# A third decay buffer that lies in SBUF, and one butterfly stage of the weight transform made by Pool

## The reference

```python
# first block, per token t, channel d, state n
dA = exp(delta[t, d] * A[d, n])
h  = dA * h + (delta[t, d] * x[t, d]) * B[t, n]
y[t, d] = sum_n h[d, n] * C[t, n]
# second block
x = fwht(x * SU_ug) / 64
x_up   = x @ W_up.T   * (Wscale_ug[:2048] * 64)
x_gate = x @ W_gate.T * (Wscale_ug[2048:] * 64)
x = silu(x_gate) * x_up
x = fwht(x * SU_dp) / 64
x = x @ W_down.T * (Wscale_dp * 64)
```

## Time and profile before

| | us |
|---|---|
| median of 3 runs (2644.28 to 2645.57) | 2645.28 |
| the profiled execution | 2648.76 |
| its span, first instruction to last | 2647.0 |
| first scan starts, last scan starts | 70.7, 2466.7 |
| PE busy | 2574.1 (97%) |
| DVE busy | 2243.8 (85%) |
| POOL busy | 2046.4 (77%) |
| ACT busy | 1815.0 (69%) |

### The profile page before, as it was taken

How to read it: one execution, slowest core, us unless ns; L and a number is a source line. 1 busy time by engine, 2 the same in 40 slices (tenths; PEclk the granted TensorE clock), 3 DMA queues, 4 the chain that set the end, 5 groups by cost and what they waited for, 6 DMA issues and landing times.

```text
span 2647.0 us, 46296 instructions
## 1 busy us (share of the span) xinstructions
PE 2574.1 (97%) x16048; PEld 2187.0 (83%) x16048; DVE 2243.8 (85%) x2573; ACT 1815.0 (69%) x3935; POOL 2046.4 (77%) x1691
## 2 busy tenths in 40 slices
PE   7999989999999999999999999999999999989998
PEld 5566668989888888989888898989888898978888
DVE  6898998899898898899899889989889889889522
ACT  4776777677777777777777767777777777755322
POOL 6776879788787979888797979888797988877222
PEclk9999999999999999999999999999999999989999
DMA  5654256657666666666666665766666666646675
GB/s 181 214 204 167 100 166 219 224 196 241 210 236 215 216 221 209 238 204 232 220 224 221 215 225 199 240 212 227 225 216 221 207 221 214 224 176 230 239 288 190
DMA packets 165209, 564.41 MB, mean 213 GB/s; under 512 B 17264, under 2 KB 19696, under 8 KB 132976
## 3 DMA queue, kind: packets, MB, share of 16 engines
q1 hardware_dynamic: 164976, 561.44, 61.5%
HBM read 527.30 MB, written 34.08 MB: 212 GB/s over the span
## 4 chain that ended last, share of the span: by engine, by line
PE 78%; DVE 10%; ACT 7%; issue 3%; DMA 1%; POOL 0%; SPq 0%; DVEq 0%; ACTq 0%; POOLq 0%
PE pF L726 21%; PE hT L633 14%; PE pM L651 13%; PE pD L742 10%; PE pM L703 8%; DVE h L1180 5%; DVE acc L1193 3%; PE pM L673 3%; PE pD L766 3%; ACT decay L986 2%; PE decay L726 2%; PE hT L625 1%; PE pF L766 1%; ACT delta L963 1%; ACT delta L958 1%
## 5 line engine op out<-in xcount | busy, mean ns | idle before, releaser
L1180 DVE TENSOR_TENSOR_SCAN h<-decay,dbx 128x512 f32<-128x512 f32 x1024 | 1200.1, 1206 | 73.7 <-ACT decay L986 41.5
L1362 POOL TENSOR_TENSOR dbx<-u,bb 128x2048 f32<-128x2048 f32 (+1 forms) x272 | 1179.6, 4338 | 37.5 <-DVE h L1180 35.5
L986 ACT ACTIVATE decay<-delta,a_neg 128x255 f32<-128x255 f32 x2048 | 874.0, 468 | 301.8 <-DVE h L1180 295.0
L1193 DVE SCALAR_TENSOR_TENSOR acc<-hT,bcT,acc 128x1024 f32<-128x1024 f32 x480 | 610.3, 1271 | 141.1 <-PE hT L633 137.5
L726 PE MATMUL pF<-fxT_hi,wug 128*128 128x256 f32 x3712 | 725.3, 288 | 0.7 <-issue 0.7
L726 PEld LDWEIGHTS pF<-fxT_hi,wug 128*128 128x128 f32 x3712 | 595.9, 192 | 1.3 <-issue 1.1
L633 PEld LDWEIGHTS hT<-ident,h 128*128 128x128 f32 x4096 | 472.8, 141 | 140.8 <-issue 89.5
L633 PE MATMUL hT<-ident,h 128*128 128x128 f32 x4096 | 535.4, 274 | 33.3 <-DVE acc L1193 22.1
L726 PE MATMUL pF<-fxT_lo,wug 128*128 128x256 f32 x1856 | 525.7, 283 | 0.0
L651 PE MATMUL pM<-xnT,w_in 128*128 128x256 f32 x2016 | 479.9, 381 | 4.1 <-ACT hid L906 2.6
L651 PEld LDWEIGHTS pM<-xnT,w_in 128*128 128x128 f32 x2016 | 367.3, 191 | 51.6 <-issue 5.0
(11 more groups left out here) (177 smaller groups left out, 2674.9 us busy)
## 6 DMA issues: line engine op xcount, KB each, us to landing
wug<-scratch_ug SPq DMA_DIRECT2D x243, 1024.0 KB, 4.8
wd<-scratch_wd SPq DMA_DIRECT2D x243, 512.0 KB, 4.1
w_in<-in_W_in SPq DMA_DIRECT2D x252, 256.0 KB, 2.9
bb<-scratch_bc SPq DMA_DIRECT2D x128, 256.0 KB, 4.7
xb<-in_hidden_states SPq DMA_DIRECT2D x16, 512.0 KB, 5.2
xr<-in_hidden_states SPq DMA_DIRECT2D x16, 512.0 KB, 5.8
out<-xr SPq DMA_DIRECT2D x15, 512.0 KB, 3.7
kept_ug<-scratch_ug SPq DMA_DIRECT2D x7, 1024.0 KB, 8.0
```

The source lines that it names most:

```text
L986: e = act.activation(da[q % 2][:, i, 1:], delta[c % 2][:, dt, 1:], ACT.Exp, scale=a_neg[:, dt, n:n + 1])
L1180: dve.tensor_tensor_scan(row(h[n % 2][:, tiles, :]), row(da[q % 2][:, :, :]), row(dbx[n % 2][:, tiles, :]), 0.0, ALU.mult, ALU.add).then_i ...
L1193: dve.scalar_tensor_tensor(acc[c % 2][:, tb, :], hT[:, :], cn, acc[c % 2][:, tb, :], ALU.mult, ALU.add).then_inc(acc_done, 1)
L1362: pool.tensor_tensor(dbx[n % 2][:, tiles, :], u[:, tiles, :], rows, ALU.mult).then_inc(done if restarts(c) else prod_done, 1)
```

## The change

There are two parts. The first is in `exps` and `scan`: the list `da` gets a third buffer `decay2`, which is made with `sb` and so lies in SBUF, and the quarters go to the three buffers in turn over all states, so that ACT may be three quarters ahead. The room for it comes from `dt_rows` and `dtin`, which now lie in the buffer `tap[0]`. The second part is in the weight transform. The order of `GROUPS` changes (up 0, all of down, then the rest). The first two up groups are made as before (`WHOLE`). For the six others (`SUMMED`) POOL makes the sum and the difference of tiles 0, 1 and 2, 3, in two instructions of 128x1024 from one input buffer into another (`half_sums`), and PE then needs 2 matmuls a row and not 4. The table `room` is changed to match.

```diff
-        dt_rows = sb("dt_rows", [P, TB, DTR])
-        dtin = sb("dtin", [P, T])
+        dt_rows = tap[0][:, 0, :].rearrange("p (a k) -> p a k", a=TB)
+        dtin = tap[0][:, 1, :]
...
-        da = [pb(f"decay{i}", [P, DQ, T]) for i in range(2)]
+        da = [pb(f"decay{i}", [P, DQ, T]) for i in range(2)] + [sb("decay2", [P, DQ, T])]
+
+        def da_of(c, n, q):
+            return da[(NQ * (NST * c + n) + q) % len(da)]
...
-        IN_BUF = dict(zip(UG_GROUPS, (0, 0, 0, 1, 2, 0, 1, 2)))
+        IN_BUF = dict(zip(UG_GROUPS, (0, 0, 1, 0, 2, 1, 0, 2)))
+        WHOLE, SUMMED = UG_GROUPS[:2], UG_GROUPS[2:]
+        SUM_BUF = dict(zip(SUMMED, (2, 1, 0, 2, 1, 0)))
+        LAST_USER = dict(zip(UG_GROUPS, [None, WHOLE[0], LAST_DOWN, WHOLE[1]] + SUMMED))
...
-        steps_of = lambda o: 2 if GROUPS[o // KT][0] == "down" else KT
+        steps_of = lambda o: KT if o // KT in WHOLE else 2
+        FIRST_SUM = 18
...
-                room = (4 if k == 0 or 8 <= k < 16 else 3 if 23 <= k < 28 else 2) if c == 0 else 2
+                at = SLOTS * c + k
+                room = (4 if k == 0 else 3 if k >= 8 else 2) if at < FIRST_SUM else (2, 1, 1)[(at - FIRST_SUM) % 3]
...
+                            for new in [i for i in SUMMED if LAST_USER[i] == o // KT]:
+                                HAD_LOAD[divmod(at + 1, SLOTS)].append(new)
+                                HAD_ADD[divmod((at + 5) // 2 * 2, SLOTS)].append(new)
...
-                    if c == 0 and n == 0 and q < 2:
-                        act.wait_ge(da_zeroed, 2)
+                    if c == 0 and n == 0 and q < len(da):
+                        act.wait_ge(da_zeroed, len(da))
                     else:
-                        act.wait_ge(scan_done, NQ * (NST * c + n) + q - 1)
+                        act.wait_ge(scan_done, NQ * (NST * c + n) + q - len(da) + 1)
...
-                        e = act.activation(da[q % 2][:, i, 1:], delta[c % 2][:, dt, 1:], ACT.Exp, scale=a_neg[:, dt, n:n + 1])
+                        e = act.activation(da_of(c, n, q)[:, i, 1:], delta[c % 2][:, dt, 1:], ACT.Exp, scale=a_neg[:, dt, n:n + 1])
...
-                dve.tensor_tensor_scan(row(h[n % 2][:, tiles, :]), row(da[q % 2][:, :, :]), row(dbx[n % 2][:, tiles, :]), 0.0,
+                dve.tensor_tensor_scan(row(h[n % 2][:, tiles, :]), row(da_of(c, n, q)[:, :, :]), row(dbx[n % 2][:, tiles, :]), 0.0,
...
+            def half_sums(g):
+                src, dst = had_in[IN_BUF[g]], had_in[SUM_BUF[g]]
+                pool.wait_ge(had_loaded[IN_BUF[g]], 16 * (in_use(g) + 1))
+                if SUMMED.index(g):
+                    pool.wait_ge(had_halved, 2 * SUMMED.index(g))
+                pool.tensor_tensor(dst[:, 0:2, :], src[:, 0:2, :], src[:, 2:4, :], ALU.add).then_inc(had_halved, 1)
+                pool.tensor_tensor(dst[:, 2:4, :], src[:, 0:2, :], src[:, 2:4, :], ALU.subtract).then_inc(had_halved, 1)
...
+                for g in HAD_ADD.get((c, k), ()):
+                    half_sums(g)
```

More of the change, by code:

```diff
@@ L166, in fused_block @@
         w_out_in = sem("w_out_in"); down_in = [sem("down_in0"), sem("down_in1")]; wscale_in = sem("wscale_in")
-        had_loaded = [sem(f"had_loaded{i}") for i in range(len(had_in))]
+        had_loaded = [sem(f"had_loaded{i}") for i in range(len(had_in))]; had_halved = sem("had_halved")
         had_setup = sem("had_setup"); w_first_in = sem("w_first_in"); diag_done = sem("diag_done"); turned_dve = sem("turned_dve"); turned_pool = sem("turned_pool")
@@ L288, in fused_block @@
         POOL_ADDS = {5: (0,), 6: (1, 2), 7: (3, 4), 8: (5, 6), 9: (7,)}
-        GROUPS = ([("up", 0), ("down", 0), ("up", 1)] + [("down", q) for q in range(1, KT)] + [("up", q) for q in range(2, KT)]
-                  + [("gate", q) for q in range(KT)])
+        GROUPS = ([("up", 0)] + [("down", q) for q in range(KT)] + [("up", q) for q in range(1, KT)] + [("gate", q) for q in range(KT)])
         LAST_DOWN = max(g for g, (name, q) in enumerate(GROUPS) if name == "down")
@@ L300, in split_use @@
             return SETS[:g].count(SETS[g])
-        IN_BUF = dict(zip(UG_GROUPS, (0, 0, 0, 1, 2, 0, 1, 2)))
+        IN_BUF = dict(zip(UG_GROUPS, (0, 0, 1, 0, 2, 1, 0, 2)))
+        WHOLE, SUMMED = UG_GROUPS[:2], UG_GROUPS[2:]
+        SUM_BUF = dict(zip(SUMMED, (2, 1, 0, 2, 1, 0)))
+        LAST_USER = dict(zip(UG_GROUPS, [None, WHOLE[0], LAST_DOWN, WHOLE[1]] + SUMMED))
         def in_use(g):
             return [IN_BUF[i] for i in UG_GROUPS if i < g].count(IN_BUF[g])
-        def next_in(g):
-            return [i for i in UG_GROUPS if i > g and IN_BUF[i] == IN_BUF[g]][:1]
         def split_row(s, o):
@@ L322, in had_scale @@
             return row_scale[:, KT * GROUPS[g][1] + r:KT * GROUPS[g][1] + r + 1] if GROUPS[g][0] == "down" else su_ug[:, r:r + 1]
-        HAD_PE, HAD_EVAC, HAD_STORE, HAD_LOAD = ({(c, k): [] for c in range(2) for k in range(SLOTS)} for i in range(4))
-        steps_of = lambda o: 2 if GROUPS[o // KT][0] == "down" else KT
+        HAD_PE, HAD_EVAC, HAD_STORE, HAD_LOAD, HAD_ADD = ({(c, k): [] for c in range(2) for k in range(SLOTS)} for i in range(5))
+        steps_of = lambda o: KT if o // KT in WHOLE else 2
+        FIRST_SUM = 18
         HAD_EVAC[0, 0] += [3]
@@ L470, in load_had @@
                 name, q = GROUPS[g]
-                older = [i for i in UG_GROUPS if i < g and IN_BUF[i] == IN_BUF[g]]
-                if older or IN_BUF[g]:
-                    wait_first(sp, had_mm, KT * ((older[-1] if older else LAST_DOWN) + 1), sp_passed)
+                if LAST_USER[g] is not None:
+                    wait_first(sp, had_mm, KT * (LAST_USER[g] + 1), sp_passed)
                 sp.dma_start(had_in[IN_BUF[g]][:, :, :], W[f"W_{name}"].rearrange("(k p) f -> p k f", p=P)[:, :, DM * q:DM * (q + 1)]
@@ L758, in had @@
                         pe.wait_ge(had_lo, o - len(had_bank) + 1)
-                    if g in UG_GROUPS and r == 0:
+                    if g in WHOLE and r == 0:
                         pe.wait_ge(had_loaded[IN_BUF[g]], 16 * (in_use(g) + 1))
-                if g in UG_GROUPS:
+                    if g in SUMMED and r == 0:
+                        pe.wait_ge(had_halved, 2 * (SUMMED.index(g) + 1))
+                if g in WHOLE:
                     src, last, minus = had_in[IN_BUF[g]][:, i, :], i == KT - 1, (r & i).bit_count() % 2
+                elif g in SUMMED:
+                    src, last, minus = had_in[SUM_BUF[g]][:, r // 2 * 2 + i, :], i == 1, r % 2 * i
                 else:
```

4 lines of the change are left out of this document (1 added, 3 removed).

## The result

| | us | against before |
|---|---|---|
| before | 2645.43 (2643.74 to 2646.28, 6 runs) | |
| changed | 2971.62 (2970.4 to 2973.82, 6 runs) | 1.1233, 95% interval 1.1221 to 1.1245 |
| forecast | 2900 (2720 to 3010) | |

The change costs 326 us, 12%. The forecast had the sign and most of the size, 255 us; it is 71 us short.

The account below looks back on a forecast made before the run. PE, busy 97%, looked like the bound, with DVE and POOL close to full. Held scans +280, decays -25 and transform 0 made +255 on 2648.76: 2904, as a median 2900 us, range 2720 to 3010.

Parts of the forecast that it names:

- The mechanism: Scans from `decay2`, with two SBUF inputs, wait for the whole POOL instruction under way; POOL's next waits up to 1.17 us.
- Rival (a): Scans from SBUF aren't held and stay at about 1.17 us: -20, so 2625 us; chance 0.13.
- The waits: 341 scans from SBUF each wait 1.27 us on average for POOL: 434 us, 27 us a chunk.
- the states that I worked out: States 12 to 14: waits of 2.3 us in 13, 3.0 in 14, nothing in 12's third quarter.
- Rival (b): Most SBUF scans settle into POOL's gaps and idle time takes most of the rest: +6 a chunk, 2740 us; chance 0.16.
- How much idle time takes up: Per chunk, waits less DVE idle time: +4 in tap states, +13.5 in the other eleven, +17.5 together, +280 us in all.
- the tap states: States 4 to 8, where POOL adds the taps: 8.5 us of waits meet 5.7 idle, POOL is the bound, +4 a chunk.
- POOL's side: POOL's instructions wait behind SBUF scans, 25 us a chunk against 24.5 idle; `dbx` grows from 4.60 by up to 1.2 us.
- rival (c): POOL becomes the bound as well and both engines' delays feed each other: all 434 us paid, 3060 us; chance 0.13.
- The decays: Scans' waits for ACT's decays, 41.5 us before: ACT a quarter further ahead gains 25 us, within 0 and 41.5.
- all but vanish: The expected sign that DVE's waits for ACT's decays, 41.5 us before, nearly disappear.
- The transform: Passes 0 and 1: PE loses 41.3 us of work, POOL gets 28.7; effect 0, between -30 and +15 us.

Follow-up runs that it names:

- the small kernel: A separate kernel with only scans and POOL instructions: scans with two SBUF inputs take 5.33 us beside POOL's tensor_tensor, 1.224 us alone.
- the run with the third quarter: The changed kernel with the SBUF buffer in the third quarter of every state only, 256 scans: 2749.57 us.
- The fillers: The kernel before plus unused bn_stats on DVE, all decays in PSUM: 2841.9 us at every third scan, 2920.76 us at the measured waits.
- the replay: The kernel before plus unused DVE work as each scan was held with the third buffer alone: 2920.76 us; with POOL's held time too, 2950.13 us.
- the even filler: The kernel before, all decays in PSUM, plus two unused bn_stats on DVE ahead of every third scan: 2841.9 us.
- the full replay: The kernel before plus unused work on DVE and POOL as each was held with the third buffer alone: 2950.13 us.

## Why the forecast was right, and where it fell short

**The mechanism** is shown, in the kernel and in isolation. The step from tensor_tensor in the earlier trace rows to the scan, which no row of before had, holds: the small kernel and all 235 held scans go by the same rule. It is the rule of the Trainium skill too, in "SBUF — State Buffer", section "Who interferes with whom": two SBUF inputs of DVE collide with an instruction of GpSimd that reads SBUF, "not with one that only writes it". Both halves agree with the small kernel, 5.33 us beside tensor_tensor and 1.224 beside memset. Rival (a) is out.

**The waits**: 341 x 1.27 = 434 us were forecast, 462 came (1697 us for all scans less 1235). That it came so close is partly luck. I divided by the span of the scans before, 2397 us; over the changed kernel's own, 2719 us, the same sum gives 1.12 us a scan and 383 us, or 398 with `xr` and the new sums, which I had left out. By this estimate the scans met POOL at a somewhat worse phase than a random one, and the two errors nearly cancelled. Of the states that I worked out, the waits of 2.3 and 3.0 us measured 2.0 and 2.9 (4.29 and 5.23 us for the pairs that took 2.33); the third quarter of state 12, which I put at nothing, waited 0.5. Rival (b) expected the step to settle in POOL's gaps; it didn't, and the run with the third quarter shows that it takes a place in the state, chosen on purpose, to bring the wait down to 0.9.

**How much idle time takes up**: I said 27.1 a chunk less 9.6, +17.5, and 1.6 off for the decays, +15.9. Measured were 27.6 less 7.6, +20.0 in passes 6 to 14. The 7.6 hold the decays' gain too, so they stand against 9.6 + 1.6 = 11.2 forecast. This is the term that was mis-sized: over passes 3 to 14 it makes 48 of the 71 us. In the tap states of pass 6, answering to the earlier trace rows:

```profile
1137.82:1190.83 53.01, 48.24 (x283) 37.48 (x282) 50.60 (x48) 36.61 (x86) 49.35 (x46) 1.00 0.53 181
```

The stretch grew by 5.7 us where I had +4. I had POOL as the bound there; it isn't alone, with 2.4 us of idle time left on DVE and 3.7 on POOL. The fillers say why so little idle time counts: the same 436 to 442 us of work cost 195 us when spread evenly and 276 at the places of the waits, in pieces of up to 4.5 us.

**POOL's side** I had as a rival (c) with all 434 us paid. It is real and smaller: 29 us by the replay. It doesn't lie where I looked for it: the `dbx` of 128x2048, which I had growing by up to 1.2 us, went from 4597 to 4634 ns on average.

**The decays**: I took 25 us of gain. Scans still wait 33.3 us for decays, 8 less than before, and "all but vanish" was wrong. Half, 16.8 us, still lie at the third quarters of states 9 and 14, behind ACT's long instructions; 13.0 us are new, in states 7 and 8, where ACT's exponentials stand behind instructions that themselves wait for POOL's taps.

**The transform**: the value 0 within -30 and +15 held, but for the reason that I gave only in part. With the held scans it costs 10 us, and without them it gives nothing either, where I had up to 29.6 of gain. DVE's idle time in passes 0 and 1 did not go with PE's work: it moved to the next wait. Passes 0 and 1 grew by 50 us together where two of my chunks make 32: 18 more of the missing 71, about half of them the transform (pass 0 takes 167.6 us with it and 160.3 without). The last 5 lie between the profiled executions, 322 us apart in span, and the medians.

## What to carry to other kernels

Before a buffer goes from PSUM to SBUF, count for each DVE instruction that reads it how many of its inputs will lie in SBUF; with two, a first price for each is the sum of half the squares of POOL's SBUF-reading instructions over the span, and POOL pays up to the length of the scan. The place in the state moved that price from 0.9 to 1.7 us here. A wait that lands in bursts costs more than its sum less the idle time: here idle time took up over half of 436 us of added work when it came evenly, and a good third of 442 us when it came as the waits do. And an engine at 97%, with 78% of the chain, gave nothing when it was relieved, since others stood just behind it: read what each of them waits for before counting the gain.

## What I had not expected of the hardware

DVE and POOL take strict turns even when both have work queued: in the small kernel five scans and five POOL instructions alternate, 5.33 and 5.30 us each. So POOL's short instruction behind a long one is held for a scan as a long one would be: 128x8 columns went from 212 to 688 ns on average.

TensorE's granted clock fell in most of the kernels in which PE had to pause more. In pass 1 its mean was 1.00 before (2.4 GHz throughout), 0.94 with the transform alone, where PE has 42 us less of the transform to do in two passes, and 0.84 in the changed kernel, where PE was busy 128 of 173 us and waited for DVE in the pauses; a mean in between is a mixture with 1.2 GHz. Over the whole span it was 0.969 in the changed kernel, 0.977 with the third buffer alone, also 0.977 in the replay, which has no collision, and 0.996 with the even filler. So it doesn't need the collision: it fell where DVE was delayed in bursts, and not where the same delay came evenly. What it costs I could not separate; it isn't what the third buffer costs above the full replay, whose clock, 0.975, is nearly the same.
